# Routed attention: sums over values behind the scores of the even instead of the odd heads

## What is computed

```python
def heavy_attn(xq, ctx, scores_kv, rms_g, w_q, w_kv, null_kv, w_out):
    xq, ctx = rmsnorm(xq, rms_g), rmsnorm(ctx, rms_g)
    q = (xq @ w_q).reshape(b, -1, HEADS, DH).transpose(0, 2, 1, 3)
    kv = jnp.einsum('bni,ihd->bhnd', ctx, w_kv)
    k, v = kv[..., :DH], kv[..., DH:] * scores_kv[:, None, :, None]
    k, v = with_null_row(nk, k), with_null_row(nv, v)      # one learned null key and value per head
    attn = jax.nn.softmax(jnp.einsum('bhqd,bhkd->bhqk', q * DH ** (-0.5), k), axis=-1)
    o = jnp.einsum('bhqk,bhkd->bhqd', attn, v)
    return o.transpose(0, 2, 1, 3).reshape(b, -1, HDH) @ w_out
```

## Time and profile before

| What | Value |
|---|---|
| Median of 3 runs | 4286.02 us (4284.94 to 4286.93) |
| Profiled execution, its own time | 4281.34 us |
| Its span | 4279.6 us |
| Mean granted clock of TensorE | 0.97 of full |
| TensorE matmuls busy | 3973.7 us (93%) |
| VectorE busy | 2820.8 us (66%) |
| ScalarE busy | 1786.0 us (42%) |
| GpSimd busy | 877.2 us (20%) |

### The profile page before, as it was taken

One profiled execution on the slowest core, in us unless ns is written; L12 is line 12 of the kernel. 1 busy time (PEld: TensorE's weight loads), 2 busy tenths in 40 slices (PEclk: granted clock), 3 DMA queues, 4 the chain that ended last, 5 costly groups with the idle time before them and its releaser, 6 DMA issues. The chain is left out here.

```text
span 4279.6 us, 96921 instructions
## 1 busy us (share of the span) xinstructions
PE 3973.7 (93%) x39328; PEld 3279.4 (77%) x39328; DVE 2820.8 (66%) x5012; ACT 1786.0 (42%) x4746; POOL 877.2 (20%) x663
## 2 busy tenths in 40 slices
PE   6788869999999999989999999968999999999998
PEld 5677757888888888878888888857677677677776
DVE  9888857776766767665555566674755646646546
ACT  7434324344433434434444433222544534534434
POOL 0222202222222222222222222211111011111011
PEclk9899979999999999999999999988999999999999
DMA  9688752222223222211222111122012022022021
GB/s 318 168 231 233 208 173 74 83 93 85 82 85 95 83 83 88 86 50 61 67 64 61 60 60 60 45 87 60 19 43 58 9 55 51 16 53 51 16 45 14
DMA packets 341371, 360.91 MB, mean 84 GB/s; under 512 B 23104, under 2 KB 237376, under 8 KB 340928
## 3 DMA queue, kind: packets, MB, share of 16 engines
q1 hardware_dynamic: 262592, 287.52, 22.5%
q0 software_dynamic: 12288, 33.56, 3.7%
q10 hardware_dynamic: 66048, 33.56, 2.9%
HBM read 228.21 MB, written 76.02 MB: 71 GB/s over the span
## 5 line engine op out<-in xcount | busy, mean ns | idle before, releaser
L1684 POOL TENSOR_TENSOR l_prob<-l_prob,l_inv 128x768 f32<-128x768 f32 x256 | 389.6, 1543 | 1690.9 <-DVE l_inv L1641 1690.9
L1235 ACT ACTIVATE l_prob<-l_ps_s,l_neg_max 128x192 f32<-128x192 f32 x1024 | 420.7, 443 | 7.5 <-DVE l_neg_max L1617 7.3
L2237 ACT ACTIVATE h_prob<-h_ps_s,h_neg_max 128x1024 f32<-128x1024 f32 x256 | 285.6, 1116 | 253.4 <-DVE h_neg_max L2311 253.4
L1617 DVE TENSOR_REDUCE l_neg_max<-l_ps_s 128x4 f32<-128x768 f32 x256 | 233.1, 952 | 238.5 <-PE l_ps_s L1004 219.4
L2308 DVE TENSOR_REDUCE h_neg_max<-h_ps_s 128x1 f32<-128x1024 f32 x256 | 312.3, 1220 | 99.7 <-PE h_ps_s L2100 91.0
L2365 DVE COPY h_probs_t<-h_ps_t 128x512 f32<-128x512 f32 x256 | 176.4, 689 | 143.1 <-PE h_ps_t L2112 142.9
L2127 PEld LDWEIGHTS h_ps_o<-h_probs_t,ahead_then_values 128*64 128x64 f32 x4096 | 221.6, 137 | 44.1 <-issue 43.0
L2127 PE MATMUL h_ps_o<-h_probs_t,ahead_then_values 128*64 128x128 f32 x4096 | 252.5, 276 | 0.0
L2112 PEld LDWEIGHTS h_ps_t<-ident,h_prob 64*128 64x128 f32 x4096 | 152.2, 140 | 121.7 <-ACT h_prob L2237 61.0
L1235 ACT ACTIVATION_READ_ACCUMULATOR l_prob<-l_ps_s,l_neg_max 128x1 f32 x1024 | 235.8, 230 | 0.0
L1004 PEld LDWEIGHTS l_ps_s<-l_k_t,l_q_t 64*64 64x64 f32 x6144 | 189.1, 133 | 48.1 <-issue 44.8
(11 more groups left out here) (392 smaller groups left out, 10793.2 us busy)
## 6 DMA issues: line engine op xcount, KB each, us to landing
toep_back<-taps_padded ACTq DMA_DIRECT2D x32, 1024.0 KB, 10.3
x<-xg SPq DMA_DIRECT2D x64, 512.0 KB, 8.7
l_xin<-x SPq DMA_DIRECT2D x128, 256.0 KB, 3.3
l_xres<-x SPq DMA_DIRECT2D x128, 256.0 KB, 3.2
l_val_side<-l_val SPq DMA_DIRECT2D x256, 128.0 KB, 3.1
out_dram<-l_res SPq DMA_DIRECT2D x128, 256.0 KB, 2.0
ahead_then_values<-x SPq DMA_DIRECT2D x126, 256.0 KB, 3.1
xin<-in_L_attn_x_dram SPq DMA_DIRECT2D x32, 768.0 KB, 6.3
```

Of the source, the lines that this page charges most:

```text
L1235: last = nc.scalar.activation(prob[t % 2][:, h, pair, :], ps_s[:, h, pair, BOTH], ACT.Exp, bias=neg_max[:, t % 2, h, pair:pair + 1], accum ...
L1617: nc.vector.tensor_reduce(neg_max[:, t % 2, h, :], ps_s[:, h, :, BOTH], AX_X, ALU.max, negate=True).then_inc(max_made, 1)
L1684: nc.gpsimd.tensor_tensor(mine, mine, spread(inv[:, t % 2, h, :], [1, PAIRS], [0, WIN + P]), ALU.mult).then_inc(p_normed, 1)
L2237: nc.scalar.activation(prob[i % 2][:, :].rearrange("p (a k) -> p a k", a=2), ps_s[i % 2][:, :, :], ACT.Exp, bias=neg_max[:, qt % 2, h:h + ...
```

## The change

The loops on TensorE and VectorE run over pairs of steps, with j from 0 to 16 and i = 2j. TensorE's order in an iteration becomes: turn i, scores i + 2, at j % 4 = 0 the null turn, the sums of pair j - 1, the turn of the reciprocals (j % 4 = 0) or the projection (j % 4 = 1), turn i + 1, scores i + 3. VectorE: copy i, maximum i + 2, then reciprocals (j % 4 = 3), division (j % 4 = 1) or result (j % 4 = 2), copy i + 1, maximum i + 3, then the null difference (j % 4 = 2), `normalise` in iterations j = 11 to 14, add null (j % 4 = 0). ScalarE's loop is written from exponential 1 on, with copy i ahead of exponential i + 2, which is the order that it had; only the exponential of the null difference comes one iteration earlier. GpSimd and SyncE are untouched, and so is every computation.

```diff
@@ -2182,24 +2182,31 @@
                             if t == 0 and g == 1:
                                 turn_null_rows(b)
                     scores(b, 1)
-                    for i in range(STEPS + 2):
+                    for j in range(STEPS // 2 + 1):
+                        i, qt = 2 * j, j // PAIRS
                         if i < STEPS:
                             turn_probs(b, i)
                         if i + 2 < STEPS:
                             scores(b, i + 2)
                         elif i < STEPS and after:
-
                             for n in range(2):
-                                turn_rows(b + 1, (i + 2 - STEPS) * 2 + n)
-                        if i % HEADS == 0 and i > 0:
-                            turn_null(b, i // HEADS - 1)
-                        if i >= 3 and i % 2 == 1:
+                                turn_rows(b + 1, n)
+                        if j % PAIRS == 0 and j > 0:
+                            turn_null(b, qt - 1)
+                        if j >= 1:
                             for half in range(2):
-                                attend(b, (i - 2) // 2, half)
-                        if i % HEADS == 1 and i > HEADS:
-                            turn_inv(b, i // HEADS - 1)
-                        if i % HEADS == 2 and i > HEADS:
-                            project_out(b, i // HEADS - 1)
+                                attend(b, j - 1, half)
+                        if j % PAIRS == 0 and j > 0:
+                            turn_inv(b, qt - 1)
+                        if j % PAIRS == 1 and j > 1:
+                            project_out(b, qt - 1)
+                        if i < STEPS:
+                            turn_probs(b, i + 1)
+                        if i + 3 < STEPS:
+                            scores(b, i + 3)
+                        elif i < STEPS and after:
+                            for n in range(2, GT):
+                                turn_rows(b + 1, n)
 
                 for n in range(GT):
                     turn_rows(0, n)
@@ -2257,23 +2264,24 @@
                             act.wait_ge(projected, b * 20 + g * 8 + t + 1)
                             nc.scalar.activation(val[:, (g - 1) * GT + t, :], bank(t), ACT.Identity,
                                                  scale=entry("factor", b, g * GT + t)).then_inc(v_kept, 1)
+                    exponential(b, 1)
                     for i in range(STEPS):
-                        if i + 1 < STEPS:
-                            exponential(b, i + 1)
+                        qt = i // HEADS
                         act.wait_ge(pt_made, 2 * (b * STEPS + i) + 2)
                         if i >= 4:
                             act.wait_ge(attended, b * STEPS + i // 2 * 2 - 2)
                         nc.scalar.activation(probs_t[i % 4][:, :, DH:], ps_t[1][:, :, :],
                                              ACT.Identity).then_inc(pt_kept_act, 1)
-                        if i >= STEPS - 2 and after:
+                        if i % HEADS == 0 and i > 0:
+                            keep_null(b, qt - 1)
+                        if i + 2 < STEPS:
+                            exponential(b, i + 2)
+                        elif after:
                             for n in range(2):
                                 keep_rows(b + 1, (i + 2 - STEPS) * 2 + n)
-                        if i % HEADS == HEADS - 2:
-                            qt = i // HEADS
+                        if i % HEADS == HEADS - 3:
                             act.wait_ge(gap_made, b * QB + qt + 1)
                             nc.scalar.activation(null_exp[:, qt % 2, :], null_gap[:, qt % 2, :], ACT.Exp).then_inc(null_exp_made, 1)
-                        if i % HEADS == 0 and i > 0:
-                            keep_null(b, i // HEADS - 1)
                     keep_null(b, QB - 1)
 
                 for n in range(GT):
@@ -2309,6 +2317,12 @@
                                             negate=True).then_inc(max_step, 1)
                     v.wait_ge(max_step, b * STEPS + i + 1)
                     nc.vector.tensor_tensor(at, at, neg_null[:, qt, h:h + 1], ALU.min).then_inc(max_made, 1)
+
+                def keep_probs(b, i):
+                    v.wait_ge(pt_made, 2 * (b * STEPS + i) + 1)
+                    if i >= 4:
+                        v.wait_ge(attended, b * STEPS + i // 2 * 2 - 2)
+                    nc.vector.tensor_copy(probs_t[i % 4][:, :, 0:DH], ps_t[0][:, :, :]).then_inc(pt_kept_dve, 1)
 
                 def keep_result(b, qt):
                     v.wait_ge(out_made, b * QB + qt + 1)
@@ -2357,38 +2371,42 @@
                                 keep_rows_lo(b, n)
                     for i in range(2):
                         maximum(b, i)
-                    for i in range(STEPS + 2):
+                    for j in range(STEPS // 2 + 1):
+                        i, qt = 2 * j, j // PAIRS
                         if i < STEPS:
-                            v.wait_ge(pt_made, 2 * (b * STEPS + i) + 1)
-                            if i >= 4:
-                                v.wait_ge(attended, b * STEPS + i // 2 * 2 - 2)
-                            nc.vector.tensor_copy(probs_t[i % 4][:, :, 0:DH], ps_t[0][:, :, :]).then_inc(pt_kept_dve, 1)
-                        if i % HEADS == 2 and i > HEADS:
-                            divide(b, i // HEADS - 1)
+                            keep_probs(b, i)
                         if i + 2 < STEPS:
                             maximum(b, i + 2)
-                        if after and STEPS - HEADS <= i < STEPS - HEADS + GT:
-                            normalise(b + 1, i + HEADS - STEPS)
-                        if after and STEPS - 2 <= i < STEPS:
+                        elif i < STEPS and after:
                             for n in range(2):
-                                keep_rows_lo(b + 1, (i + 2 - STEPS) * 2 + n)
-                        qt = i // HEADS
-                        if i % HEADS == HEADS - 3 and i < STEPS:
-
-                            v.wait_ge(max_made, b * STEPS + i + 3)
-                            nc.vector.tensor_tensor(null_gap[:, qt % 2, :], neg_max[:, qt % 2, :], neg_null[:, qt, :],
-                                                    ALU.subtract).then_inc(gap_made, 1)
-                        if i % HEADS == HEADS - 1 and i < STEPS:
+                                keep_rows_lo(b + 1, n)
+                        if j % PAIRS == 3:
                             v.wait_ge(null_exp_made, b * QB + qt + 1)
-                            v.wait_ge(exp_made, b * STEPS + i + 1)
+                            v.wait_ge(exp_made, b * STEPS + i + 2)
                             nc.vector.tensor_tensor(inv[:, qt % 2, :], total[:, qt % 2, :], null_exp[:, qt % 2, :],
                                                     ALU.add).then_inc(inv_step, 1)
                             v.wait_ge(inv_step, (b * QB + qt) * 2 + 1)
                             nc.vector.reciprocal(inv[:, qt % 2, :], inv[:, qt % 2, :]).then_inc(inv_step, 1)
-                        if i % HEADS == 1 and i > HEADS:
+                        if j % PAIRS == 1 and j > 1:
+                            divide(b, qt - 1)
+                        if j % PAIRS == 2 and j > 2:
+                            keep_result(b, qt - 1)
+                        if i < STEPS:
+                            keep_probs(b, i + 1)
+                        if i + 3 < STEPS:
+                            maximum(b, i + 3)
+                        elif i < STEPS and after:
+                            for n in range(2, GT):
+                                keep_rows_lo(b + 1, n)
+                        if j % PAIRS == 2:
+
+                            v.wait_ge(max_made, b * STEPS + i + 4)
+                            nc.vector.tensor_tensor(null_gap[:, qt % 2, :], neg_max[:, qt % 2, :], neg_null[:, qt, :],
+                                                    ALU.subtract).then_inc(gap_made, 1)
+                        if after and 0 <= j - (STEPS // 2 - 1 - GT) < GT:
+                            normalise(b + 1, j - (STEPS // 2 - 1 - GT))
+                        if j % PAIRS == 0 and j > 0:
                             add_null(b, qt - 1)
-                        if i % HEADS == 3 and i > HEADS:
-                            keep_result(b, qt - 1)
 
                 for n in range(GT):
                     normalise(0, n)
```

## The result

| | before | changed |
|---|---|---|
| Median | 4285.48 us (4283.35 to 4286.93) | 4328.67 us (4326.20 to 4330.84) |
| Profiled execution, its span | 4279.6 us | 4326.3 us |
| Mean granted clock | 0.97 | 0.968 |

The ratio is 1.0087, with a 95% interval of 1.0072 to 1.0103. The change makes the kernel slower by 0.9%, 43 us. The direction was forecast; the time lies above the range of 4295 to 4322, and the loss was put at 25 us.

The account below looks back on a forecast made before the run. TensorE sets the pace and no second engine is full, so order decides. 26.6 + 6.3 + 1.0 - 0.6 - 8.6 = +24.7 us takes the profiled 4281.34 to 4306.0; 4.7 for the median gives 4311, range 4295 to 4322.

Parts of the forecast that it names:

- (a): TensorE's sums over the values one step earlier: no new wait, and no copy waits for buffers; 0.
- (c): VectorE's close: sums 7 now end before maximum 19 starts, division goes behind maximum 20; no time of its own.
- (d): Walk of one quarter (8 steps) on TensorE: 26.02 us, 1.11 more than 24.91; 24 quarters give +26.6 us.
- (b): ScalarE, GpSimd and SyncE: the null gap's earlier exponential is covered by sums, GpSimd's null part is asked for earlier; 0.
- bare place: A turn right behind scores on TensorE, with nothing between; claimed to bind by up to 0.55 us unless filled.
- (e): Normalising the next sequence's rows on VectorE, now behind four odd maxima, was to cost 7 x 0.90 = +6.3 us.
- (f): Tail of a sequence, turns 28 to 31: +1.0 us over seven sequences, -0.6 us in the last.
- (g): Head of a sequence, turns 0 to 4: turn 3 no longer waits; -1.3 us in five, -0.7 in three, together -8.6.
- the sums cover the division: Rival: sums ahead of the projection hide its wait for the division; faster, 4276 us, chance 0.07.
- the clock falls at the projection: Rival: the new 1.31 us wait ahead of each projection lowers the granted clock; 41 us more, 4352 us, chance 0.05.
- only parities are exchanged: Rival: turns wait no more than before, the projection's wait grows by 0.3 us; no difference, 4288 us, chance 0.08.
- the chain's 5.23: Maximum, copy, exponential, ScalarE's copy, then the second next turn: 5.23 us, against 4.68 of TensorE's work per pair.

Follow-up runs that it names:

- e1: The changed kernel with ScalarE's exponential of the null difference put ahead of the exponential it stood behind; 4310.46 us, ratio 1.0060 to the kernel before.
- e6: The changed kernel with VectorE's division alone moved ahead of maximum 20, add null left in place; 4313.72 us, ratio 1.0059 to the kernel before.
- e2: The changed kernel with add null on VectorE ahead of copy i + 1 and the division ahead of maximum 20; 4285.94 us, ratio 1.0002 to the kernel before.
- e3: The kernel before with VectorE's division moved behind maximum i + 2 instead of ahead of it; 4351.10 us, ratio 1.0153 to the kernel before.
- e4: The changed kernel with each pair's sums cut in two halves and the division ahead of maximum i + 2; 4275.16 us, ratio 0.9978 to the kernel before.

## Why the prediction was wrong, point by point

**What bounds the kernel.** Right. TensorE sets the pace, its waits are order, and the lags taken from a quarter of before give e1's quarter to 0.01 us.

**(a), (c), (d): the quarter.** The order of waits was right and its size nearly so: 26.02 walked, 26.36 measured, 26.01 in e1. Two things were lacking. One is the step of the next paragraph. The other: step (d) did not see that sums 8 wait for add null, because they begin to write the PSUM tile that add null reads; the code shows it (`attend` waits on `o_read`), and the walk had sums 8 start at 19.18 without looking. It did not change the result: the projection is bound by the division, which stands behind the same add null on VectorE, so the 0.69 us were part of the 1.31 and not on top of it. It would have changed it in a kernel whose division is early: e6.

**(b) and (d): GpSimd at nothing, maximum 16 at the usual lag.** This is the step that failed in the quarters. (b) said that GpSimd's null part is asked for earlier and took that at 0; (d) then gave maximum 16 the lag of 1.45, in which the small step counts 0.16. Neither laid GpSimd's multiplication, 1.04 us, over that step. The step took 0.50, in a bare place where all of it counts: 24 x 0.35 = 8.4 us (shown by e1), of the 8.9 by which the quarters missed. The row of before was there to read: the same step took 0.26 in the quarter walked. The Trainium skill has a rule for this (SBUF — State Buffer, section "Who interferes with whom"): a VectorE instruction with two inputs in SBUF contends with a GpSimd instruction that reads SBUF. SBUF is the memory in which the tiles lie that are not in PSUM. The trace agrees: the small step reads two SBUF operands and was held, the maximum before it reads PSUM and took its usual 1.22 under the same multiplication. When the step came, 0.48 us of the multiplication were left, and it ended 0.02 after them. An estimate from these rows: a step that came as the multiplication began would lose up to about 0.9 us.

**(e): normalising.** Right for the quarter: the third quarters take 26.81 instead of 26.36, which is the 0.45 walked. What it cost in the tail does not stand apart from (f).

**(f): tail.** Turn 28 to the next turn 0 takes 81.38 instead of 80.98, +0.40, seven times; (e) and (f) together had +0.60. Good to 1.1 us in the sum with the last sequence.

**(g): heads.** The mechanism was right, the size was off. Turn 0 to 4 takes 10.25 at full clock in sequence 0 of the changed kernel, 10.31 walked. But only that head ran at full clock; the other seven took 11.26 to 13.14, against three slow ones of eight before. In e1 and e2, whose heads have the same instructions in the same order, five and four of eight took 10.25 or 10.26; in e6 and in the changed kernel's second trace (r2) none did. Turn 3 waits for nothing in all eight, as forecast. The head of sequence 5 in the changed kernel on TensorE answers to the earlier trace rows:

```profile
3865.38 0.66 PE L2112 MATMUL h_ps_t<-ident,h_prob 64*128 64x64 f32 x16
...
3868.88 1.12 PE L2112 MATMUL h_ps_t<-ident,h_prob 64*128 64x64 f32 x16 [2.08 <-ACT h_probs_t L2273]
...
3871.15 1.06 PE L2112 MATMUL h_ps_t<-ident,h_prob 64*128 64x64 f32 x16
...
3876.64 0.71 PE L2112 MATMUL h_ps_t<-ident,h_prob 64*128 64x64 f32 x16 [0.40 <-ACT h_probs_t L2273]
```

The wait of 2.08 us ahead of turn 1 was there before as well; now the turn behind it runs at the lower level (1.12 us instead of 0.71). The step that failed is the assumption that five heads stay clean. I do not know what decides it. The slow heads of before are the same three in both executions although these start 16.7 us apart, but the changed kernel's head of sequence 0 was clean (10.25) in one execution and slow (11.80) in the other, which started 0.2 us apart. Nothing run here moves the head's wait itself.

**The rivals.** That the sums cover the division came true only where the close was moved ahead (e2), by the very point that was named, one or two maxima; even there the time was that of before (1.0002), not faster. That the clock falls at the projection is excluded for the changed kernel by a clock of 1.00 (in all 24 places the projection's matmuls take 3.70 us), and shown for a wait of 2.16 us by e3. That only parities are exchanged fell for this change, whose close stands late; with the close ahead (e2) it is nearly so, 0.13 us a quarter. (The row that the prediction set against it, 3200.63 to 3205.84, is 5.21, not the chain's 5.23 exactly; the argument does not hang on it.)

**The range.** Its upper end left out that a cover taken at nothing could fail (8.4 us) and that any head could go slow (up to 5 x 1.3), and it took the median's scatter of several us as none. Its margin above the forecast, 11 us, had no room for both the collision (8.4) and the heads (5.0), and scatter ahead of turn 0 came on top. By its own terms the lower end would have been about 4292, not 4295.

## What to carry to other kernels

Where steps of several engines are reordered, lay the instructions of every other engine, in their new places, over the short instructions of the critical chain: here 1.04 us of GpSimd cost 0.35 us a quarter through a step of 0.16. A short instruction that takes longer in some places than in others (0.26 against 0.16 before the change) is the sign to look for. When work is put ahead of a waiting instruction as a cover, the steps that feed this instruction must move ahead too, or they stand behind the same long neighbours. And sums of uneven pieces leave bare places; cutting them in halves (e4) gave more than choosing which of the two places to leave bare.

## What the runs showed of the hardware

A VectorE step of 128 x 1 elements with two SBUF operands took 0.50, 0.37 and 0.26 us instead of 0.16 (changed kernel, e4, before), each time ending 0.02 us after a GpSimd multiplication. Beside a wait of TensorE of 2.16 us (e3) the granted clock fell in half of 24 like places and 8 matmuls took 5.26 instead of 3.70 us; beside waits of 0.69 and 0.51 us with 1.9 us of matmuls between them it did not. A wait of 2.08 us ahead of turn 1 stood in every head, and the clock fell in three of eight (before), seven (changed kernel) or all eight (r2). Everything ahead of the routed attention ended anywhere from 2993 to 3010 us after the start in ten traces of programs that are the same up to there, while the 1286 us behind it repeated to 0.2.
